# A two-layer graph network on one core: relation products moved ahead of the adjacency product

## What is computed

```python
h = maximum(layernorm(x), 0)                       # 625 x 512
xr = einsum('nd,rde->rne', h, W_rel)               # three relations
agg = segment_sum(xr[edge_type, src] + b_rel[edge_type], dst)
h_self = einsum('nd,tde->tne', h, W_self)[node_type, arange(N)] + b_self[node_type]
x = x + relu(h_self + agg)
h = maximum(layernorm(x), 0)
Q, K, V = split(h @ W_qkv.T + b_qkv)               # 8 heads of 64
out = attention over the edges (softmax per receiver and head)
x = x + out @ W_ff.T + b_ff
```

## Time and profile before

| | us |
|---|---|
| median of 3 runs (lowest to highest) | 316.27 (316.02 to 317.65) |
| the profiled execution's own time | 315.79 |
| its span, first to last instruction | 314.0 |
| PE, DVE, ACT, POOL busy | 290.9, 199.1, 143.8, 71.4 |

### The profile page before, as it was taken

One profiled execution on the slowest core, in us unless ns is written; L12 is line 12 of the kernel. 1 busy time (PEld: TensorE's weight loads), 2 busy tenths in 40 slices (PEclk: granted clock), 3 DMA queues, 4 the chain that ended last, 5 costly groups with the idle time before them and its releaser, 6 DMA issues.

```text
span 314.0 us, 5396 instructions
## 1 busy us (share of the span) xinstructions
PE 290.9 (93%) x1966; PEld 227.1 (72%) x1966; DVE 199.1 (63%) x481; ACT 143.8 (46%) x282; POOL 71.4 (23%) x98
## 2 busy tenths in 40 slices
PE   2848799999999999999899999999799999999995
PEld 1513244544677788678787889999699998999984
DVE  5899977996133344334457942884987758576742
ACT  1151344432325422524434442677877666665731
POOL 7038004210483234620002410420001102020202
PEclk9999999999999999999999999999999999999999
DMA  5672697111162400042500000000000100000001
GB/s 184 230 238 83 242 370 274 61 41 38 38 229 76 134 3 3 2 134 78 191 0 0 2 0 3 0 0 3 0 2 0 37 2 0 37 0 35 3 33 32
DMA packets 10970, 22.29 MB, mean 71 GB/s; under 512 B 950, under 2 KB 966, under 8 KB 10938
## 3 DMA queue, kind: packets, MB, share of 16 engines
q1 hardware_dynamic: 8772, 16.80, 15.8%
q10 hardware_dynamic: 1366, 2.45, 2.3%
q0 software_dynamic: 800, 2.62, 2.2%
HBM read 15.60 MB, written 6.26 MB: 70 GB/s over the span
## 4 chain that ended last, share of the span: by engine, by line
PE 79%; DVE 12%; ACT 3%; DMA 2%; issue 2%; DVEq 0%
PE banks L1260 14%; PE banks L1206 9%; PE banks L1246 9%; PE banks L1151 8%; PE banks L1348 7%; PE banks L1332 7%; PE banks L1104 6%; PE banks L1321 6%; PE banks L1370 4%; DVE key_hot L835 3%; DVE row_hot L842 2%; DMA raw<-in_L_gnn_W_qkv_dram 2%; PE banks L1236 1%; PE banks L1193 1%; PE banks L1360 1%
## 5 line engine op out<-in xcount | busy, mean ns | idle before, releaser
L1104 PE MATMUL banks<-key_hot,row_hot 128*128 128x480 f16 x120 | 33.1, 426 | 8.5 <-DVE key_hot L835 8.5
L1018 DVE CUSTOM_DVE_ANT_0 s_sb<-banks,mask_add 128x640 f32<-128x640 f32 x40 | 32.6, 821 | 13.1 <-PE banks L1321 13.0
L675 ACT ACTIVATE p_sb<-s_sb,neg_max 128x640 f32<-128x640 f32 x40 | 32.9, 824 | 12.5 <-DVE neg_max L1018 12.2
L835 DVE TENSOR_SCALAR key_hot<-iota,picked 128x480 f16<-128x480 f16 x120 | 36.8, 373 | 0.0
L1206 PE MATMUL banks<-adjT,h 128*128 128x320 f16 x240 | 33.1, 299 | 0.4 <-DVE zT_even L894 0.4
L1104 PEld LDWEIGHTS banks<-key_hot,row_hot 128*128 128x128 f16 x120 | 12.8, 107 | 26.3 <-DVE key_hot L835 9.2
L1206 PEld LDWEIGHTS banks<-adjT,h 128*128 128x128 f16 x240 | 23.3, 98 | 9.8 <-DVE zT_even L894 0.7
L1332 PE MATMUL banks<-ident,p_sb 128*128 128x128 f32 x200 | 29.8, 275 | 0.3 <-ACT pT L682 0.2
L1260 PE MATMUL banks<-w_hl,zT_even 128*128 128x512 f32 x120 | 29.3, 394 | 0.0
L505 POOL TENSOR_TENSOR msgT<-msg_f,msgT 128x128 fp32r<-128x128 f32 x20 | 8.6, 461 | 90.3 <-ACT msgT L696 90.3
L1321 PE MATMUL banks<-k_hi,q_st 128*128 128x320 f32 x80 | 26.8, 343 | 2.0 <-DVE neg_max L1018 2.0
(11 more groups left out here) (179 smaller groups left out, 473.6 us busy)
## 6 DMA issues: line engine op xcount, KB each, us to landing
w_self<-in_L_gnn_W_self_dram SPq DMA_DIRECT2D x3, 1024.0 KB, 10.5
raw<-in_L_gnn_W_rel_dram SPq DMA_DIRECT2D x3, 1024.0 KB, 14.7
raw<-in_L_gnn_W_qkv_dram SPq DMA_DIRECT2D x3, 1024.0 KB, 5.2
sorted_rows<-zero_rows ACTq DMA_DIRECT2D x1, 1792.0 KB, 11.6
self_rows<-hs SPq DMA_DIRECT2D x7, 256.0 KB, 2.2
hs<-sorted_rows SPq DMA_DIRECT2D x1, 1280.0 KB, 7.2
xs<-in_x_dram SPq DMA_DIRECT2D x1, 1024.0 KB
raw<-in_L_gnn_W_ff_dram SPq DMA_DIRECT2D x1, 1024.0 KB, 5.2
```

The costliest lines, as they stand in the source:

```text
L675: nc.scalar.activation(p_sb[:, n % NPR, :], s_sb[:, n % NS, :], ACT.Exp, scale=-1.0, bias=neg_max[:, it, h:h + 1], accum_out=denom[:, it, ...
L835: return nc.vector.tensor_scalar(to_key, iota[:], float(KEYS * w), key, ALU.add, ALU.is_equal)
L1018: nc.vector.tensor_tensor_reduce(s_sb[:, n % NS, :].rearrange("p (a j) -> p a j", a=2), banks[:, c:c + 2, 0:HALF], mask_add[:, it, :].rear ...
L1104: mm(banks[:, w % 2, 0:KEYS], row_hot[:, w % 2, k, :], key_hot[:, w % 2, k, :], start=(k == 0), stop=True, skip_group_check=True).then_inc ...
```

## The change

The factors change places: `y = h W_r + b_r` is made first, and the adjacency is applied to y.

- h is transposed on PE (`turn`, five units) and split into high and low 32-bit parts `hT`. A `y` unit is 13 matmuls of 512 columns (12 products and one that adds the relation's bias); ACT and DVE split it into `y_hl`. There are 15 of them: those of relation 0 stand between windows 0 and 4, those of relation 1 between windows 4 and 9, and those of relation 2 after the second adjacency product.
- The self products (`sturn`, `self`) follow relation 1: they begin after window 9 and end after the last window. The tiles `hs` have three places instead of seven, so SP loads tile t+3 only when tile t has been stored back.
- The adjacency of a relation is copied by DVE to 32 bits (`conv`, 3200 elements a partition, three times). An `agg` unit is ten matmuls of 512 columns into banks 0 to 4. The `z`, `gemm` and `cnt` units go; two small `types` units count node types alone.
- W_0 is loaded on ACT's queue at the very start, while x is loaded, and W_1 behind x. POOL makes the low parts of both before it scatters the sorted rows. W_2 is loaded when the last self tile has been stored.
- The loads of the layer-2 weights begin after the second adjacency product. Of the 16 `wt` units, ten now stand in the loop over `sum` and `ln`, two for each tile; before, the loop had two.
- ACT makes a 32-bit copy of the residual for every `agg` unit (`res32`), which PE uses only where a window spans more than 16 chunks of edges.
- `take_bank` waits for DVE where DVE reads the unit, and for ACT otherwise. The empty DVE instruction that freed the bank of each K and Q unit goes.

```diff
-        schedule = [("cnt", 0, 0), ("cnt", 1, 0)] + z_units(0) + z_units(1)
+        schedule = [("turn", 0), ("turn", 1), ("y", 0, 0), ("win", 0), ("turn", 2), ("y", 0, 1), ("turn", 3), ("win", 1),
+                    ("turn", 4), ("y", 0, 2), ("win", 2), ("y", 0, 3), ("win", 3), ("y", 0, 4)]
         for it in range(NT):
-            schedule += [("gemm", 0, it), ("m", it, 0), ("m", it, 1)]
-        schedule += z_units(2)
-        wt_units = [("wt", g, kt) for g in range(3) for kt in range(KD)]
+            schedule += [("win", 4 + it), ("y", 1, it)]
+        schedule += [("win", 9), ("sturn", 0), ("sturn", 1)]
+        for t in range(SORTED):
+            schedule += [("win", w) for w in (10 + 2 * t, 11 + 2 * t) if w < NW]
+            schedule += [("all",), ("types", 0), ("types", 1), ("conv", 0), ("conv", 1)] * (t == (NW - 10) // 2)
+            schedule += [("self", t)] + [("sturn", t + 2)] * (t + 2 < SORTED)
         for it in range(NT):
-            schedule += [("gemm", 1, it)] + wt_units[3 * it:3 * it + 3]
-        schedule += [("wt", 3, 0), ("wt", 3, 1)]
+            schedule += [("agg", 0, it), ("m", it, 0), ("m", it, 1)]
+        schedule += [("agg", 1, it) for it in range(NT)]
+        wt_units = [("wt", g, kt) for g in range(4) for kt in range(KD)]
+        schedule += [("conv", 2), ("y", 2, 0), ("y", 2, 1)]
+        for it in range(2, NT):
+            schedule += [("y", 2, it)] + wt_units[2 * (it - 2):2 * (it - 1)]
         for it in range(NT):
-            schedule += [("gemm", 2, it), ("sum", it)]
+            schedule += [("agg", 2, it), ("sum", it)]
             if it >= 2:
                 schedule.append(("h2T", it - 2, 0))
             schedule.append(("ln", it))
-            if it == 0:
-                schedule += [("wt", 3, 2), ("wt", 3, 3)]
+            schedule += wt_units[6 + 2 * it:8 + 2 * it]
...
# ACT, at the start
+            act.dma_start(w_raw[0][:], wrel_d[0].rearrange("(k p) n -> p k n", p=P)).then_inc(s_wrel[0], 16)
...
+            weights_hi(0, 0)
+            standard_deviation(0, 0, 2, 1)
+            weights_hi(0, 1)
+            rows0(0)
+            rows0(1)
...
# PE
+                elif kind == "y":
+                    _, r, it = u
+                    pe.wait_ge(s_ufree, dve_done[("turn", it)])
+                    n = 0
+                    for kt in range(KD):
+                        if it == 0:
+                            pe.wait_ge(s_wlo, KD * r + kt + 1)
+                        for pl, w in ((0, w_hi[r]), (1, w_hi[r]), (0, w_lo[r])):
+                            mm(b, hT[:, pl, kt, it * P:(it + 1) * P], w[:, kt, :], start=(n == 0), stop=False)
+                            n += 1
...
+                    ins = mm(b, sel6[:, r, :], bhl[:], start=False, stop=True)
...
+                pairs = [(jt, p) for jt in range(NT) for p in range(2)]
...
+                        ins = mm(banks[:, it, :], adj[:, jt, c0:c0 + P], y_hl[r % 2][:, p, jt, :], start=False,
+                                 stop=(stop and n == len(pick) - 1), skip_group_check=True)
...
+                add(adj32[r], it * P, pairs[:-1], False)
...
# SP
+            for t in range(SORTED):
+                sp.wait_ge(s_uhi, act_done[("self", t)])
+                sp.dma_start(self_d[t * P:(t + 1) * P, :], hs[:, t % 3, :]).then_inc(s_kept, 16)
+                if t + 3 < SORTED:
+                    sp.wait_ge(s_kept, 16 * (t + 1))
+                    sorted_rows(t + 3)
```

More of the change, by code:

```diff
@@ L140, in gnn_kernel @@
[L140 to L143, removed]
-        adjT = place("adjT", o_r4 + 10240, [P, NT, R, NP], F16)
-        adjT_res = place("adjT_res", o_r4 + 29440, [P, NT, R, NP], F8)
+        o_y, o_w, o_r4, o_ss = 20480, 61440, 92160, 157696
+        hT = place("hT", 0, [P, 2, KD, NP], F32R)
@@ new lines, in gnn_kernel @@
+        y_hl = [place("y_even", o_y, [P, 2, NT, D], F32R), place("y_odd", o_y + 20480, [P, 2, NT, D], F32R)]
+        W_AT = [(o_w, o_w + 8192), (o_r4 + 29440, o_w + 16384), (o_w + 18944, o_w + 10752)]
+        w_raw = [place(f"w_raw{r}", W_AT[r][0], [P, KD, D], F32) for r in range(R)]
+        w_lo = [place(f"w_lo{r}", W_AT[r][0], [P, KD, D], F32R) for r in range(R)]
+        w_hi = [place(f"w_hi{r}", W_AT[r][1], [P, KD, D], F32R) for r in range(R)]
+        in0 = place("in0", o_r4, [P, NT, D], F32)
@@ L291, in gnn_kernel @@
         schedule += [("q", a, half) for a in range(KD) for half in range(2)]
-        ring = [u for u in schedule if u[0] not in ("gemm", "sum", "ln")]
+        ring = [u for u in schedule if u[0] not in ("win", "all", "conv", "agg", "sum", "ln")]
         number = {u: n for n, u in enumerate(ring)}
@@ L296, in bank @@
             return banks[:, 5 + number[u] % 3, :]
[L298 to L308, removed]
+        act_units = [u for u in ring if u[0] in ("turn", "y", "sturn", "self", "wt", "h2T", "q", "k")]
         act_done = {u: n + 1 for n, u in enumerate(act_units)}
+        dve_units = [u for u in ring if u[0] in ("turn", "y", "types", "m", "wt", "h2T", "v")]
+        dve_done = {u: n + 1 for n, u in enumerate(dve_units)}
         m_units = [u for u in ring if u[0] == "m"]
@@ L474, in _ @@
                                              ).then_inc(s_self, 16)
-            for kt in range(KD):
-                weights_lo(1, kt)
             for n, u in enumerate(m_units):
@@ L480, in _ @@
                 c0, cn = m_cols(part)
+                if part == 1 and it < KD:
+                    weights_lo(2, it)
                 pool.wait_ge(s_ln, n + 1)
[L482 removed]
+                pool.wait_ge(s_ufree, dve_done[u])
                 nc.gpsimd.tensor_tensor(mask_add[:, it, c0:c0 + cn], mask_add[:, it, c0:c0 + cn],
                                         mlog[:, n % 2, 0:cn], ALU.subtract).then_inc(s_mask, 1)
[L485 to L486 removed]
             for it in range(NT):
@@ L811, in masks @@
                 dve.wait_ge(s_type, 1 + T)
-                for g in range(3):
+                for g in range(2):
                     nc.vector.tensor_copy(mask6[:, :, g * BG + R:g * BG + R + T], type_mask[:]
@@ L1214, in unit @@
+                elif kind == "types":
+                    c0, cn = m_cols(u[1])
+                    pe.wait_ge(s_keys, MASKS)
+                    for it in range(c0 // P, (c0 + cn) // P):
+                        ins = mm(b[0:BROWS, it * P - c0:(it + 1) * P - c0], mask6[:, it, :], ident16[:],
+                                 start=(it * P == c0), stop=True, skip_group_check=True)
                 elif kind == "m":
@@ new lines, in aggregate @@
+                add(adj32[r], it * P, pairs[-1:], r == R - 1).then_inc(s_agg, 1)
+            for u in schedule:
+                if u[0] in ("conv", "sum", "ln"):
+                    continue
+                if u[0] == "win":
+                    w = u[1]
+                    first_chunks(w)
+                    if w == 6:
+                        pe.wait_ge(s_bias, BIASES_IN)
+                        nc.tensor.transpose(banks[:, 2, 400:400 + 3 * KD], bqkv_r[:], ident[0:3 * KD, 0:3 * KD]
+                                            ).then_inc(s_prep, 1)
+                    if w == 9:
+                        pe.wait_ge(s_keys, EDGE_KEYS)
+                        pe.wait_ge(s_place, 2)
+                        widest = pe.value_load(bounds[0:1, 2, NW:NW + 1], min_val=1, max_val=EC)
+                        _, offsets = nc.values_load_multi_w_load_instructions(
+                            tile_off_i[0:1, 0:SORTED], engines=(pe.engine,), min_val=0, max_val=(T - 1) * KD * D,
+                            skip_runtime_bounds_check_because="the vector engine worked them out")
+                elif u[0] == "all":
+                    all_chunks()
+                elif u[0] == "agg":
+                    aggregate(u[1], u[2])
+                else:
+                    unit(u)
```

554 lines of the change are left out of this document (257 added, 297 removed).

## The result

The changed kernel takes 331.51 us, median of 4 runs (330.86 to 332.90), against 316.14 for the kernel before on the same chip (315.98 to 317.65, 4 runs): ratio 1.0487, 95% interval 1.0463 to 1.0511. I forecast 320.0 and a range to 325.0. The sign and the loop that I blamed were right; the size was 11.5 us too small.

The account below looks back on a forecast made before the run. PE was taken as the bound (79% of the span, DVE 12%). Terms 22.8 + 80.4 + 48.9 + 0.1 + 32.6 = 184.8 against 181.3, tail unchanged at 132.7, gave span 317.5 and forecast 320.0 us; range 314.5 to 325.0.

Parts of the forecast that it names:

- 13 matmuls at 0.228 = 2.97: Price of one y unit on PE, bias matmul included, from a 12-matmul product of 2.74 to 2.76 us.
- stretch 2: From the first y unit to the last self product: PE work sums to 80.4 us, ending at 103.2.
- stretch 3: From the last self product to the first sum of layer 1: 48.9 us, first sum at 152.2.
- The count matmul: Adjacency products before the first sum: 0.30 us each, five times with ten matmuls and mask counts, 17.2 us.
- Stretch 1: Kernel start to the end of the first y unit: unit starts at 17.2 us and is over at 22.8.
- 17.2 ... 20 if W_0 and the bias rows queued behind it come late: Start of the first y unit, the softest term: 17.2 us, with bounds 15 and 20.
- about 1 us: Before the first y unit, POOL's low parts beside DVE work could delay hT by about 1 us.
- 5.6 us at the lower level: First y unit: 13 matmuls at 0.43 us with PE at 1.2 GHz; at the upper level 3.0.
- up to four times 0.8 as a rival, 320 to 323: Self products: sorted-row tiles come late because loads wait for stores; 320 to 323 us, chance 0.12.
- one of 0.5: Before the first sum of layer 1: one PE wait of 0.5 us for the last y's low part.
- Stretch 4: Loop over sum and ln to layer 2's fourth transpose: iterations 5.73 and 5.87 us, 32.6 in all, loss 13.7.
- PE sets the pace in stretch 4: ACT and DVE overlap better in the loop: 21.0 instead of 32.6 us, total 308; chance 0.12 with combined cases.

Follow-up runs that it names:

- experiment 1: Changed kernel with the bias operands on 70 rows (zeros added) instead of 38 and one constant moved to make room: 326.32 us, ratio 1.0318 to the kernel before.
- experiment 2: Changed kernel with the bias operands on 64 rows instead of 38 and the same constant moved: 331.75 us, ratio 1.0492 to the kernel before.
- experiment 3: Changed kernel without the bias matmul in the 15 y units (output lacks the relations' biases): 325.25 us, ratio 1.0299 to the kernel before.
- experiment 5: Changed kernel with nine unused 480-column matmuls on PE ahead of the first y unit: 330.90 us, ratio 1.0461 to the kernel before.
- experiment 6: Changed kernel with bias rows loaded ahead of W_0, and window 0's one-hot rows and later x factors moved behind hT's first low part: 331.65 us, ratio 1.0476.
- experiment 4: Changed kernel with the loop's ten weight transposes placed ahead of the third adjacency product: 321.63 us, ratio 1.0175 to the kernel before.

## Why the prediction was wrong, point by point

**The y unit, "13 matmuls at 0.228 = 2.97": this step failed.** The bias matmul costs 0.43, and 0.11 more in the window behind it. I took a mean over instructions of 128 rows for one of 38, though no row of the kernel before shows a matmul on 38 rows; it shows only the count matmul on 70, at 0.30. The price was an unmeasured form and should have had bounds on both sides. The count matmul was carried over at 0.30 too, though the same line of the diff took it from 70 to 38 rows. Experiments 1, 2 and 3 give it 5.2 us of the 11.5; by the chain of experiment 1 stretch 2 is 2.6 and stretch 3 3.2 shorter. With it the forecast would have been 325.2, just past the upper end of the range.

**Stretch 1, "17.2 ... 20 if W_0 and the bias rows queued behind it come late": the bound came true, +2.3.** ACT waits for the bias rows until 12.37, and on DVE `row_hot` took 1.92 us beside POOL's low parts, the effect that I had priced for `key_hot` and, before the first unit, left to the bounds ("about 1 us"). "5.6 us at the lower level" was right (5.5). Experiments 5 and 6 show that the 2.3 would have been worth little: each has its first window 2.2 or 2.3 us earlier and its first count matmul 1.4, and the medians lie 0.6 under and 0.1 over that of the changed kernel.

**Stretch 2 and 3, the rest.** 1.7 us in stretch 2: PE waits 0.68 once for a sorted tile (I had up to four times 0.8 as a rival, 320 to 323; it came once) and 0.34 for a transposed copy; the rest are units a few hundredths over their price. The profile puts the 0.68, which ends at 95.02, down to ACT, but the bank had been free since 88.7, while the tile's load was issued at 92.24 and such a load takes some 2.6. In stretch 3 some 2.8: three waits of 0.46 to 0.55 where I had one of 0.5, the second adjacency products at 2.34 instead of 2.28 each, the first ones' cycle 0.05 over its price even on 70 rows, a pair of transposes at 1.0 instead of 0.87, and 0.25 to 0.3 in each of the three units that start behind such a wait (a product of 12 takes 3.02 there on 70 rows too). In that ring the y unit and two transposes have all three banks, so the next unit waits until DVE has emptied the y unit's. The chain of the changed kernel shows it:

```profile
150.64 0.61 ACT y_even L590
...
151.34 0.70 DVE y_even L908
...
152.08 3.04 PE banks L1202 x12
```

**Stretch 4: the loop was right, its end by luck.** Iterations to 0.03 us, DVE's idle time to 0.01, and experiment 4 moves the loss with its cause. What I missed is 1.0 us, all behind the last sum: 10.5 us from it (187.83) to the transpose (198.32) for 9.45. But I had 6.7 to the end of the last `wt` parts and then one V product of 2.75. Measured, the V products start 3.0 after the sum, with the table load and the last `ybuf` beside them, and both stand behind the wait for `h2T`, partly at the lower level: 7.5. Two wrong terms, of 3.7 and 4.7 us, nearly cancel. The rival "PE sets the pace in stretch 4" is refuted as it stood: 24.31 us of PE work in 33.60.

**What hid well.** The 32-bit copy of 3200 elements took 3.49 us (I took 3.4), and nobody waited; the tail was 132.9 for 132.7; the sorted rows' load was issued at 52.83 where I had 53.

Not settled: why the V products take anything from 7.3 to 8.5 us in kernels with the same loop.

## What to carry to other kernels

Price each matmul by a row of its own shape, rows too: an instruction made smaller may be the dearer one, and a "smaller" constant in a diff deserves its own line in the sum. In a loop where two engines hand a tile back and forth, put side work of those two engines ahead of the loop, not in it: ten small units cost 6.4 us ahead of it and 17.4 inside, 1.9 of these by the clock. A gain at the start of a kernel counts only up to the next wait that is bound to something else; here 2.2 us at one unit were 1.4 in the span and no measurable part of the median.

## What the runs showed of the hardware

- A matmul on 38 or 64 rows between matmuls on 128 has its weights loaded only when the one before is nearly through: 0.35 us of idle weight load before it and 0.43 us for the matmul, against no idle and 0.24 on 70 rows. Twenty of them cost 5.2 us.
- TensorE at 2.4 GHz took 5.74 us for 24 matmuls of 512 columns, and 7.65 after a loop in which it worked some 17 of 26 us. The granted-clock column showed this (0.50 to 0.54 from 187.8 to 194); from 19.6 to 25.1 it reads 1.00, although the first y unit took 5.5 us, against 3.4 when unused matmuls ran ahead of it.
- `row_hot` took 1.92 us on VectorE beside GpSimd's subtractions and 0.95 without; `shift`, on two and three elements a row, 0.50 and 1.02 beside them, against 0.17 for five elements in the kernel before with no subtraction beside it.
- Four loads of a few rows, queued behind a megabyte on the same queue, let their reader wait until 12.37 us; ahead of it, until 9.26.
